# Shared feed-forward layer of a graph model: up-projection as three fp32r products, its weights split chunk by chunk, GELU outputs in a ring of 18 slots

## The reference, cut to what matters

```python
def _L1_ffn_ref(x, router_w, W1, b1, W2, b2):      # x: (1, 1250, 512), layer-normed
    token_repr = x.mean(axis=1)
    logits = token_repr @ router_w.T
    probs = jax.nn.softmax(logits, axis=-1)
    topk_vals, topk_idx = jax.lax.top_k(probs, TOP_K)
    topk_vals = topk_vals / topk_vals.sum(axis=-1, keepdims=True)
    expert_weights = jnp.einsum('bk,bke->be', topk_vals, pw[topk_idx])
    h = jax.nn.gelu(jnp.einsum('bsd,edf->ebsf', x, W1) + b1[:, None, None, :], approximate=False)
    out_e = jnp.einsum('ebsf,efd->ebsd', h, W2) + b2[:, None, None, :]
    return jnp.einsum('be,ebsd->bsd', expert_weights, out_e)
```

## Time and profile before

| what | value |
|---|---|
| median of 3 runs | 2153.37 us (2150.72 to 2153.77) |
| the profiled execution | 2147.26 us |
| its span, first to last instruction | 2145.7 us |
| granted TensorE clock, mean | 0.978 of full speed |
| stretch of the last layer norm and transposes | about 1864.4 to 1882.9 us |
| turn 0 of the layer, up to the first down | 1872.4 to 1914.2 us |
| 64 pairs of up and down | 1914.2 to 2113 us |
| last 16 downs | 2113 to 2142 us |

### The profile page before, as it was taken

How to read it: one execution, slowest core, us unless ns; L and a number is a source line. 1 busy time by engine, 2 the same in 40 slices (tenths; PEclk the granted TensorE clock), 3 DMA queues, 4 the chain that set the end, 5 groups by cost and what they waited for, 6 DMA issues and landing times.

```text
span 2145.7 us, 42525 instructions
## 1 busy us (share of the span) xinstructions
PE 2036.4 (95%) x13564; PEld 1485.7 (69%) x13565; DVE 1338.3 (62%) x2651; ACT 1080.2 (50%) x2327; POOL 548.8 (26%) x567
## 2 busy tenths in 40 slices
PE   7899999999999989999999999996899999999998
PEld 4544444444444466898998999885697888778886
DVE  3311799999999977566665666665513445644444
ACT  6531244444444422777777777784343322554443
POOL 3101377777777752200000000004000000400000
PEclk9999999999999997999999999997999999999999
DMA  6652488888888875547104400045400200310000
GB/s 219 222 183 92 130 237 239 239 237 237 237 239 238 236 296 194 223 177 299 52 20 176 176 20 20 26 170 176 179 11 10 88 20 20 113 45 11 11 11 19
DMA packets 141916, 297.46 MB, mean 139 GB/s; under 512 B 28925, under 2 KB 70662, under 8 KB 137239
## 3 DMA queue, kind: packets, MB, share of 16 engines
q1 hardware_dynamic: 96933, 159.09, 21.1%
q0 software_dynamic: 36592, 130.56, 20.4%
q10 hardware_dynamic: 8322, 6.89, 1.0%
HBM read 242.31 MB, written 54.17 MB: 138 GB/s over the span
## 4 chain that ended last, share of the span: by engine, by line
PE 90%; DVE 3%; issue 2%; DMA 2%; ACT 2%; POOL 1%; DVEq 0%; ACTq 0%; POOLq 0%
PE psum L2577 15%; PE psum L2431 12%; PE psum L2394 9%; PE psum L2716 7%; PE psum L2749 5%; PE psum L2568 4%; PE psum L2567 4%; PE psum L2569 4%; PE psum L2622 4%; PE psum L2613 3%; PE psum L2419 3%; PE psum L2653 3%; PE psum L2643 3%; PE psum L2292 2%; PE psum L2667 1%
## 5 line engine op out<-in xcount | busy, mean ns | idle before, releaser
L1075 POOL DMA_INDIRECT big_b<-sender_table,wide x360 | 398.3, 1106 | 180.9 <-issue 101.6
L2431 PEld LDWEIGHTS psum<-big_b,wide 128*32 128x32 f32 x3600 | 165.1, 109 | 192.0 <-issue 102.3
L2577 PEld LDWEIGHTS psum<-xn_T,big_b 128*128 128x128 f32 x2048 | 263.0, 191 | 19.9 <-issue 0.2
L1257 ACT ACTIVATE wide<-wide 128x290 bf16<-128x290 f32 x360 | 168.5, 527 | 213.3 <-PE psum L2431 155.4
L2431 PE MATMUL psum<-big_b,wide 128*32 128x256 f32 (+2 forms) x3600 | 269.0, 386 | 0.0
L2577 PE MATMUL psum<-xn_T,big_b 128*128 128x128 f32 x2048 | 264.6, 275 | 0.0
L2394 PE MATMUL psum<-w_mlp,wide 64*128 64x512 f32 x728 | 205.3, 641 | 5.6 <-DVE big_b L1739 4.0
L1378 ACT ACTIVATE xn_T<-psum,table 128x128 f32<-128x128 f32 x368 | 135.5, 368 | 108.3 <-PE psum L2577 108.2
L1739 DVE TENSOR_TENSOR big_b<-big_b,psum 128x768 f32<-128x768 f32 x180 | 168.4, 936 | 0.0
L1738 DVE TENSOR_TENSOR big_b<-big_b,psum 128x768 f32<-128x768 f32 x180 | 167.9, 933 | 0.0
L1908 DVE TENSOR_TENSOR hid_lo<-xn_T,hid_hi 128x128 fp32r<-128x128 f32 x368 | 107.2, 291 | 97.0 <-ACT hid_hi L1378 95.4
(11 more groups left out here) (469 smaller groups left out, 3982.8 us busy)
## 6 DMA issues: line engine op xcount, KB each, us to landing
big_a<-in_L_ffn_W SPq DMA_DIRECT2D x12, 2048.0 KB, 13.0
big_b<-in_L_ffn_W SPq DMA_DIRECT2D x12, 2048.0 KB, 13.0
wide<-in_L_ffn_W SPq DMA_DIRECT2D x8, 2048.0 KB, 22.7
wide<-edge_hidden SPq DMA_DIRECT2D x91, 128.0 KB
edge_hidden<-wide SPq DMA_DIRECT2D x21, 512.0 KB, 2.9
tokens_sorted<-zeros SPq DMA_DIRECT2D x29, 256.0 KB, 3.6
adj_dram<-big_a SPq DMA_DIRECT2D x1, 6400.0 KB, 23.6
xn_T<-tokens_sorted POOLq DMA_DIRECT2D x25, 256.0 KB, 2.9
```

The costliest lines, as they stand in the source:

```text
L1075: nc.gpsimd.indirect_dma_start(out=sent[q][:, j, :], out_offset=None, in_=sender_table, in_offset=bass.IndirectOffsetOnAxis(ap=record[k][q ...
L1257: last = nc.scalar.activation(hot_step[q][:, j, :, :], block_steps[k], ACT.Sign, bias=record[k][q][:, j, Y + 1:Y + 2])
L2431: return nc.tensor.matmul(msg_psum[k].rearrange("p (c u) -> p c u", u=MUL)[bands[g], cols, :], hot_y[q][:, j, y, :], p[:, of, :], start=Fa ...
L2577: last = nc.tensor.matmul(psum[:, f % UP_BANKS, 0:P], ew1[a][:, c, f * P:f * P + P], tile_T[:, c, :], start=(c == 0), stop=(c == C - 1))
```

## The change

The up-projection is done as the down-projection is: the normed input and the weights are each split into a rounded part and a rest, and three fp32r products take the place of each fp32 one (12 instructions of 256 columns a chunk in place of 8). The input's rounded half `xt_hi` is written by ScalarE in two more copies per transposed tile, its rest `xt_lo` by VectorE in two subtractions. The weights of chunk i + 3 are split right after the GELU of chunk i: ScalarE copies them (`sw1_leading`), VectorE subtracts (`sw1_rest`), in three slots. Space for it comes from the GELU outputs: in place of two full turns (32 slots) they have a ring of 18. The one sum over the nodes becomes ten small ones, a tile each, in the loop, and UP_AHEAD goes from 4 to 3.

```diff
@@ sizes
+        SHID_RING, SHID_SLOTS, SW2_FIRST = SC + 2, 4, 9
...
+        xt_lo = xn_hi
+        SW1_SLOTS = 3
+        sw1_hi = [late_col, sw1_b[:, 0, :, :], late_out]
+        sw1_lo = [late_bl, sw1_b[:, 1, :, :], late_bk]
...
+        def shid_slot(g, j):
+            return (g * SC + j) % SHID_RING
...
-        UP_AHEAD = 4
+        UP_AHEAD = 3
@@ ScalarE
+            def sw1_leading(g, j):
+                r = hidden_rows(j)
+                i = g * SC + j
+                if i == 0:
+                    act.wait_ge(loads["sw1"], 16 * SE)
+                    filled(act, ("m5", C - 1))
+                if i >= SW1_SLOTS:
+                    filled(act, ("up", (i - SW1_SLOTS) // SC, (i - SW1_SLOTS) % SC))
+                nc.scalar.activation(sw1_hi[i % SW1_SLOTS][:, :, 0:r], sw1_cols[:, :, j * P:j * P + r], ACT.Copy).then_inc(sw1_hi_ready, 1)
+
+            def last_transposed(t):
+                full, free = filled(act, ("lastT", t))
+                parts = full.rearrange("p (c n) -> p c n", c=C)
+                nc.scalar.activation(xn_T[:, :, tile_cols[t]], parts, ACT.Copy)
+                for half, dst in enumerate((xt_hi_a, xt_hi_b)):
+                    last = nc.scalar.activation(dst[:, :, tile_cols[t]], parts[:, half * C // 2:(half + 1) * C // 2, :], ACT.Copy)
+                last.then_inc(free, 1)
+                if t < SW1_SLOTS:
+                    sw1_leading(0, t)
...
                     n, r = len(TURN_TILES[g]) * P, hidden_rows(j)
-                    if g >= 2:
-                        filled(act, ("down", TURN_TILES[g - 2][-1]))
-                    if g * SC + j >= SHID_SLOTS:
-                        act.wait_ge(shid_split, g * SC + j - SHID_SLOTS + 1)
+                    i = g * SC + j
+                    if i >= SHID_RING:
+                        g0, j0 = divmod(i - SHID_RING, SC)
+                        if j0 == SC - 1:
+                            filled(act, ("down", TURN_TILES[g0][-1]))
+                        else:
+                            act.wait_ge(sw2_used, g0 * (SC - 1) + j0 + 1)
+                    if i >= SHID_SLOTS:
+                        act.wait_ge(shid_split, i - SHID_SLOTS + 1)
                     full, free = filled(act, key)
...
+                    if i + SW1_SLOTS < TG_N * SC:
+                        sw1_leading(*divmod(i + SW1_SLOTS, SC))
@@ VectorE
+            def sw1_rest(g, j):
+                r = hidden_rows(j)
+                i = g * SC + j
+                dve.wait_ge(sw1_hi_ready, i + 1)
+                nc.vector.tensor_tensor(sw1_lo[i % SW1_SLOTS][:, :, 0:r], sw1_cols[:, :, j * P:j * P + r],
+                                        sw1_hi[i % SW1_SLOTS][:, :, 0:r].bitcast(F32), ALU.subtract).then_inc(sw1_split, 1)
+
+            def last_rest(t):
+                drained(dve, ("lastT", t))
+                settle(nc.vector.tensor_reduce(mean_parts[:, t, :], xn_T[:, :, t * P:t * P + rows(t)], AX_X, ALU.add))
+                for half, hi in enumerate((xt_hi_a, xt_hi_b)):
+                    of = slice(half * C // 2, (half + 1) * C // 2)
+                    last = nc.vector.tensor_tensor(xt_lo[:, of, tile_cols[t]], xn_T[:, of, tile_cols[t]],
+                                                   hi[:, :, tile_cols[t]].bitcast(F32), ALU.subtract)
+                last.then_inc(xt_lo_ready, 1)
+                if t < SW1_SLOTS:
+                    sw1_rest(0, t)
+
+            REST_LAG = 7
...
-            for t in range(NT):
-                drained(dve, ("lastT", t))
-            settle(nc.vector.tensor_reduce(mean_col[:, :], xn_T[:, :, 0:N], AX_X, ALU.add))
+                if t >= REST_LAG:
+                    last_rest(t - REST_LAG)
+
+            for t in range(NT + 4 - REST_LAG, NT):
+                last_rest(t)
+            settle(nc.vector.tensor_reduce(mean_col[:, :], mean_parts.rearrange("p t c -> p c t"), AX_X, ALU.add))
...
+                    if g * SC + j + SW1_SLOTS < TG_N * SC:
+                        sw1_rest(*divmod(g * SC + j + SW1_SLOTS, SC))
@@ TensorE, hidden_columns
+                pe.wait_ge(xt_lo_ready, TURN_TILES[g][-1] + 1)
+                pe.wait_ge(sw1_split, i + 1)
+                w_hi, w_lo = sw1_hi[i % SW1_SLOTS], sw1_lo[i % SW1_SLOTS]
                 for c in range(C):
-                    last = nc.tensor.matmul(out_b[0:r, 0:n], sw1_cols[:, c, j * P:j * P + r], xn_T[:, c, n0:n0 + n],
-                                            start=(c == 0), stop=(c == C - 1))
+                    hi, lo = xt_hi(c)[:, n0:n0 + n], xt_lo[:, c, n0:n0 + n]
+                    nc.tensor.matmul(out_b[0:r, 0:n], w_hi[:, c, 0:r], hi, start=(c == 0), stop=False)
+                    nc.tensor.matmul(out_b[0:r, 0:n], w_hi[:, c, 0:r], lo, start=False, stop=False)
+                    last = nc.tensor.matmul(out_b[0:r, 0:n], w_lo[:, c, 0:r], hi, start=False, stop=(c == C - 1))
```

More of the change, by code:

```diff
@@ L216, in graph_block_kernel @@
         w_mlp4 = sb("w_mlp4", [P, 4 * MUL])
+        late_out = over("late_out", 0, [P, C, P])
         w_out = sb("w_out", [P, 2, 2, MUL])
@@ L2722, in _ @@
                 transposes(("lastT", t), chunks(last_rows[:, t, :]))
-                if t == NT // 2:
-                    pe.wait_ge(loads["sw1"], 16 * SE)
-                    for u in TURN_TILES[0]:
-                        drained(pe, ("lastT", u))
                 if 0 <= t - NT // 2 < UP_AHEAD:
```

42 lines of the change are left out of this document (30 added, 12 removed).

## The result

The changed kernel takes 2163.78 us in the median of 7 runs (2160.21 to 2169.25), the kernel before 2152.07 us in 7 runs beside it (2145.49 to 2155.48). The ratio is 1.0064, 95% interval 1.0046 to 1.0082: slower by 0.64%, more than the 0.2% that a measurement can tell. The forecast was 2168.4 with a range of 2157 to 2178.

A forecast was written before the change was run, and what follows sets the result against it. TensorE, busy 95% of the span, was taken to bound the kernel. Hand-over +11, pairs +2 and ends of turns +3 make 16, rounded down to +15 on 2153.4: 2168.4 us, range 2157 to 2178.

The forecast's parts named there:

- The product: Up product on TensorE: twelve fp32r products of 256 columns take 1.47 us in place of 1.73, 0.26 less an up.
- The line through the two fp32r rows: Up product's price, from rows of 512 columns (0.233 us) and 427 on average (0.196): 0.122 us at 256.
- The rival of the dear product: Up product: narrow costs as much as wide, 0.233 each, 2.80 us an up, +97, total 2250; chance 3%.
- The pairs: Long stretch of up and down pairs: loop through ScalarE and VectorE sets 3.13 us, not 3.10; +2 us over 63.
- my 6.26: Loop over two pairs: GELU to down 3.04 us plus down to GELU 3.22; TensorE alone needs 2 x 2.84.
- Ends of turns: Turn ends: output additions and `sw1_lo` ahead of the second `w_lo` delay a down 1.3 us, three times; counted +3.
- the loop's own wait: At turn ends, the wait of the pairs' loop swallows part of the 1.3 us each, so +3 was counted.
- The hand-over: Last norms to first down: VectorE comes last, first GELU near 1893, first down at 1925, not 1914.16; +11 us.
- the sum of VectorE's 26.0 us: VectorE's loop over the last norms: statistics, roots, sums, subtractions and weights' rests, from 1866.4 to 1892.4.
- The holes: TensorE's waits before the first down: 3.3 us for `sw1_lo` of chunk 8 behind routing, 2.5 for the expert weights.
- TensorE last in the pairs: Rival in the pairs: TensorE still sets the pace, at 2.84 us; total 2148, or 2137 with up at 1.34; chance 11%.
- The cancelling case: Rival: hand-over half as dear, +6, and pairs at 3.05, -3; total within 4 us of before; chance 7%.

The follow-up runs named there:

- experiment 1: Changed kernel, in the pairs up weights split behind the next down's weights on ScalarE and VectorE: 2149.73 us, 0.9993 of the kernel before.
- experiment 2: Changed kernel with up weights split behind the next down's weights on VectorE only, ScalarE's order kept: 2165.17 us, 1.0068 of the kernel before.
- experiment 4: Changed kernel, the input tiles' rests subtracted from the transposed tile in PSUM, not its SBUF copy: 2159.13 us, 1.0038 of the kernel before.
- the last run of experiment 6: Changed kernel with down weights first, late tile splits, chunks 3 to 5 early, later additions, and routing in five pieces: 2136.71 us, 0.9933 of the kernel before.

## Why the prediction was right

The time, 2163.78, lies 4.6 us under the forecast and in its range. The mechanism was the forecast's: TensorE has less to do and waits for a queue of VectorE and ScalarE. That the number came so near is in part luck. Of one pair of profiles, the stretch up to the first down cost 3.8 us more than forecast (+14.8, not +11), and the one behind it 7.5 less (-2.5, not +5); the two misses have opposite signs. The terms came out so:

**1. The product.** 0.119 us each in the kernel whose chain is TensorE alone, 1.43 an up; forecast 0.122 and 1.47. The line through the two fp32r rows was good to 3%. The rival of the dear product is refuted: with a 128x128 load in front of each (0.19 by its record), the products still started 0.119 apart. The Trainium skill (TensorE: Matmul & The Clock Gate, "Back-to-back issue gap") gives N/2.4 + 2.5 ns, 0.109 here, which it calls the gap of a single product; this stream does not agree, as it did not at 512 columns (0.233 against 0.216). By the rule in "The mechanism" of the same page of the Trainium skill, a load overlaps a running product only if its rows of the array differ; the trace does not agree for these loads. The paragraph ahead of that rule in the section also names a background weight buffer as a way for a load to be pulled ahead, and with that the trace agrees.

**2. The pairs.** Forecast 3.13 us and +2 in all; measured 3.03, 63 x (3.03 - 3.10) = -4.4. The way was right: experiment 1 moved two instructions of it, and TensorE alone was left in the chain. Two sizes were off. Back to back on ScalarE the up's copy takes 0.52, not 0.66: I had taken the spacing of `w_hi`, which is a copy with a scale, for a copy without one. And an up is 0.04 cheaper. The two make 0.18 of the 0.21 us by which two pairs (6.05) came out under my 6.26. I had `w_lo` wait for `w_hi`; it was VectorE's `sw1_lo` that ended last, but experiment 2 shows the two ways to be equally long.

**3. Ends of turns.** Forecast 1.3 each and +3; the waits were 1.22, 1.23 and 1.21. By the spacing of the downs, an end took 1.05 us more than two pairs of its kernel, against 0.17 before, so +2.6 for three; the loop's own wait swallowed part, as forecast. Right. Pairs and ends make -1.8. Most of what is missing to -2.5 lies in the last pairs, where no up weights are left to split (spacings of 2.80 and 2.66, before 3.11 and 2.85), and in the last 16 downs, 0.2 us shorter.

**4. The hand-over.** Forecast +11, measured +14.8; this step was mis-sized by 3.8 us. The first GELU came 12.0 us later and not 8.7, the mean 33.6 behind the last attention product, where 1893.5 meant 29.8. From the first GELU to the first down I counted 32, and the profile has 32.7. So the miss lies in the sum of VectorE's 26.0 us, which in the trace were 30.85 (1870.40 to 1901.25): it took every subtraction at its undisturbed price, and four of them stood still beside GpSimd: three took 1.49 or 1.50 in place of 0.42, one of 512 columns 1.76 in place of 0.69. That makes 4.3 us, three more at 0.55 in place of 0.42 make 0.4, and the mean is 3.8 later than forecast. That these waits come from the two inputs in SBUF is shown by experiment 4; that they are worth 3.8 us at the end is not, since there only 2.0 of the first GELU came back, where one of the four was gone. The holes were 2.90 for routing (forecast 3.3) and 1.92 for the expert weights (forecast 2.5). What I gave as the cause of the hole of 2.90, the routing queued ahead of `sw1_lo` on VectorE, was not enough: the last run of experiment 6 took it away and 2.38 of 2.90 us stayed. Its timeline puts them on ScalarE, whose two table loads stand ahead of the copy; no run moved these.

**The rivals.** TensorE last in the pairs (11%) needed the loop 0.58 us shorter per two pairs than I counted (6.26). The real one was 0.2 shorter (6.05), and TensorE alone needs 5.62. The cancelling case (7%) had its pairs (-3; they gave -4.4) and was missed by the hand-over, which was dearer than counted and not half as dear. The ledger of one profile: +14.8 up to the first down and -2.5 behind it make 12.3, where the medians have 11.7.

What stays open is how much of the hand-over is TensorE's clock in the median run. I added 1.5 us for it. From the first GELU to the first down the kernel before took 29.9 us at a mean clock of 0.89, the changed one 32.7 at 0.85 or 35.3 at 0.78. From these an estimate: with the two levels of 1.00 and 0.50, TensorE stood at the lower one for 2 x 0.11 x 29.9 = 6.6 us before and for 9.8 or 15.5 after. Had TensorE been busy in all of it, half would be lost: 3.3, 4.9 and 7.8. By this estimate the clock's part of the +14.8 is about 1.6 us, near my 1.5, and the two profiles of the changed kernel should differ by 2.9, where they differ by 2.7. With the later profile the hand-over is +17.5. No experiment here held the clock fixed.

## What to carry to other kernels

When a cheaper product brings work to other engines, compute the loop that goes through them, per pair, and ask of each new instruction what is queued behind it; here the same instructions in another order took the pairs from 3.03 to 2.81 us. An instruction in the chain of waits is worth nothing if another way of the same length lies beside it, so ask where the ways part before moving one. Work that is needed late (the output additions here) belongs where its engine has slack. And of an earlier start only what arrives counts: 6.4 us at the first GELU were 2.9 at the first down in one execution. Where one profile has holes, compare the granted clock of the same stretch before a gain or loss of 3 us is put down to an edit.

## What the runs showed of the hardware

- A VectorE subtraction with two inputs in SBUF stood still while GpSimd had a multiplication or addition under way: 1.49 to 1.50 us in place of 0.42, ending about 0.3 after GpSimd's (1877.31 + 1.49, against 1877.19 + 1.33). With one input from PSUM it took 0.42, and statistics or sums with one input were not longer. GpSimd's addition that came beside the 512-column subtraction took 1.60 in place of 1.29. The Trainium skill (Trainium Architecture — The Big Picture, "What this means for kernel authors") calls the port pair that the two engines share an exclusive lock and not a split of bandwidth; with that the trace agrees: the subtraction waits until the GpSimd instruction has ended, it is not merely slowed.
- Where TensorE's stream had holes its granted clock fell, and not alike in each execution. Between the first GELU and the first down, with three holes, the same 182 or 183 instructions took 25.6 to 28.5 us of busy time in different executions, at mean granted clocks between 0.86 and 0.78, which can hide or make a difference of 3 us; in 2000 to 2030 us, where the waits were 0.2 us or none, the clock was 1.00.
- An fp32r product of 128x128 weights and 256 columns took 0.119 us in a stream at full clock, weights loaded for each; twelve of them took 1.43 us where the four plain fp32 products took 1.73.
